# ScalarE issues half of the transfers behind its own results in the first and the last chunk

## The reference

```
x  = _ln(_layernorm(x)); xn = _ln(x); dx = _shift(xn) - xn      # time mixing
r, k, v, decay, a, g from xn + dx * x_q by small matrices
step:  sa    = einsum(state, a_t)                               # 512 steps, one after the other
       state = state * d_t + sa * b_t + v_t * k_t
       o_t   = einsum(state, r_t)
o = _gn_heads(o) + bonus;  x = x + o * g @ W_o
x = x + square(relu(kf @ W_ffn1)) @ W_ffn2                      # first feed-forward
h = _layernorm(x); expert = argmax(h @ W_router)                # second: one of four experts
x = x + _layer_norm(gelu(h @ W1[expert] + b1) @ Wo + bo + h)
```

## Time and profile before

| what | us |
|---|---|
| median of 3 runs | 1193.74 |
| lowest, highest | 1191.18, 1196.12 |
| the profiled execution, its own time | 1195.53 |
| its span, first to last instruction | 1193.7 |
| TensorE busy | 1054.8 (88%) |
| VectorE busy | 940.2 (79%) |
| GpSimd busy | 650.4 (54%) |
| ScalarE busy | 605.3 (51%) |

### The profile page before, as it was taken

One profiled execution on the slowest core, in us unless ns is written; L12 is line 12 of the kernel. 1 busy time (PEld: TensorE's weight loads), 2 busy tenths in 40 slices (PEclk: granted clock), 3 DMA queues, 4 the chain that ended last, 5 costly groups with the idle time before them and its releaser, 6 DMA issues.

```text
span 1193.7 us, 19599 instructions
## 1 busy us (share of the span) xinstructions
PE 1054.8 (88%) x6099; PEld 713.3 (60%) x6099; DVE 940.2 (79%) x2283; ACT 605.3 (51%) x965; POOL 650.4 (54%) x885
## 2 busy tenths in 40 slices
PE   4676689999998999999998989999999999988976
PEld 2243356666565757666665757566666656666755
DVE  4468778898989888898988888898889888876320
ACT  2424364736465574637464564647364654733341
POOL 0246665665656656566656666665556566555200
PEclk9769899999999999999999999999999999999989
DMA  3324123342424233432424232333425233221110
GB/s 126 67 40 75 33 45 71 63 89 42 100 47 86 56 61 69 78 72 52 94 42 96 56 74 56 67 71 62 90 41 102 45 84 57 52 58 36 37 27 18
DMA packets 136496, 75.58 MB, mean 63 GB/s; under 512 B 15292, under 2 KB 129980, under 8 KB 136264
## 3 DMA queue, kind: packets, MB, share of 16 engines
q1 hardware_dynamic: 136392, 74.33, 31.0%
HBM read 11.35 MB, written 4.19 MB: 13 GB/s over the span
## 4 chain that ended last, share of the span: by engine, by line
PE 36%; DVE 20%; SPq 19%; issue 10%; ACT 8%; DMA 6%; POOL 0%; DVEq 0%; ACTq 0%; POOLq 0%
SPq L314 10%; SPq L301 6%; PE fin_b L564 6%; PE fin_a L564 5%; DMA val_rep<-val_c 5%; PE sa_ps L405 5%; DVE state L898 4%; PE mid_ps L356 4%; PE pre_a L356 3%; DVE upd L894 3%; PE var_ps L586 3%; ACT L600 3%; SPq L298 3%; DVE kv L871 2%; DVE s_a L884 1%
## 5 line engine op out<-in xcount | busy, mean ns | idle before, releaser
L1071 POOL TENSOR_TENSOR plus_kv<-state,kv 128x128 f32<-128x128 f32 x512 | 283.3, 553 | 406.1 <-DVE state L898 383.1
L405 PE MATMUL sa_ps<-s_a,con 128*128 128x128 f32 x1024 | 226.0, 303 | 55.8 <-DVE s_a L884 53.2
L405 PEld LDWEIGHTS sa_ps<-s_a,con 128*128 128x128 f32 x1024 | 172.3, 193 | 168.7 <-DVE s_a L884 137.7
L1063 POOL TENSOR_TENSOR s_r<-state,r_t 128x256 f32<-128x256 f32 x256 | 244.7, 956 | 3.3 <-DVE state L898 3.3
L894 DVE TENSOR_TENSOR upd<-sa_ps,b_t 128x128 f32<-128x128 f32 x512 | 146.2, 286 | 84.6 <-PE sa_ps L405 80.7
L898 DVE TENSOR_TENSOR state<-upd,plus_kv 128x128 f32<-128x128 f32 x512 | 191.8, 375 | 17.6
L884 DVE TENSOR_TENSOR s_a<-state,a_t 128x128 f32<-128x128 f32 x512 | 149.4, 292 | 18.5
L564 PE MATMUL fin_b<-h_e,mat 128*128 128x256 f32 x512 | 136.9, 394 | 4.0 <-ACT pick L770 4.0
L871 DVE TENSOR_TENSOR kv<-val_rep,k_t 128x512 f32<-128x512 f32 x128 | 117.8, 921 | 23.9 <-DMA val_rep<-val_c 23.3
L600 ACT ACT_TABLE_LOAD x101 | 129.6, 1283 | 1.8
L564 PE MATMUL fin_a<-h_e,mat 128*128 128x256 f32 x512 | 127.9, 379 | 0.0
(11 more groups left out here) (198 smaller groups left out, 1725.9 us busy)
## 6 DMA issues: line engine op xcount, KB each, us to landing
val_rep<-val_c SPq DMA_DIRECT2D x512, 64.0 KB, 2.4
rs_p<-row_rs SPq DMA_DIRECT2D x128, 64.0 KB, 2.1
x_in<-xT SPq DMA_DIRECT2D x16, 256.0 KB, 3.0
rs_p<-row_rk SPq DMA_DIRECT2D x64, 64.0 KB, 2.4
x_res<-xT SPq DMA_DIRECT2D x16, 256.0 KB, 3.0
rs_m<-row_frs SPq DMA_DIRECT2D x64, 64.0 KB, 2.1
rs_f<-row_ers SPq DMA_DIRECT2D x64, 64.0 KB, 2.1
rs_f<-row_lrs SPq DMA_DIRECT2D x64, 64.0 KB, 2.1
```

The source lines that it names most:

```text
L405: mm(sa_ps[:, 0:STATE], k("sum8"), s_a[:], start=True, stop=True).then_inc(s["sa"], 1)
L1063: tt(part, states, r.unsqueeze(2).broadcast_to([128, 2, N, B]), ALU.mult).then_inc(s["s_r"], 1)
L1071: tt(plus_kv[:, (t % 2) * STATE:(t % 2 + 1) * STATE], st(t), kv[:, at:at + STATE], ALU.add).then_inc(s["plus_kv"], 1)
```

## The change

Every chunk gets a set `by_act`. In chunk 0 it holds rs0, rs1 and rep, in the last chunk ers and lrs, in all others nothing. For a name in the set, SyncE issues only the first half of the DMAs: quarters 0 and 1 of a row of scales, and the first four of the eight of quarter 0 of the values. The second half is issued by ScalarE, from its own queue, right behind the instruction that wrote the row, or val_c. ScalarE waits first for its own result's semaphore and, for the scales, for the last reader of the buffer that is to be overwritten. The number of transfers, their sizes, and the semaphores that their readers wait for stay as they are.

```diff
+        self.by_act = {"rs0", "rs1", "rep"} if off == 0 else {"ers", "lrs"} if off == CHUNKS - 1 else set()
...
                 sp.wait_ge(s["row_" + name], now)
-                for g in range(4):
+                for g in range(2 if name in c.by_act else 4):
...
                 sp.wait_ge(s["val_c"], now)
-                for i in range(N):
+                for i in range(N // 2 if q == 0 and "rep" in c.by_act else N):
...
                 f(row[name][:], row[name][:], ACT.Exp, scale=-0.5).then_inc(s["row_" + name], 1)
+                if name in c.by_act:
+                    to, read, back = {"rs0": (rs_p, "kk", 1), "rs1": (rs_p, "xh0", 0),
+                                      "ers": (rs_f, "lxh", 1), "lrs": (rs_f, "h", 0)}[name]
+                    if c.has(back):
+                        act.wait_ge(s[read], (c + -back).count())
+                    act.wait_ge(s["row_" + name], c.count())
+                    for g in (2, 3):
+                        rows = row[name][32 * g:32 * g + 32, :].unsqueeze(1).broadcast_to([32, 4, QCOLS])
+                        nc.scalar.dma_start(to[:, g * QCOLS:(g + 1) * QCOLS], rows).then_inc(s[name], 16)
...
                     f(val_c[:], pre_a[:], ACT.Identity).then_inc(s["val_c"], 1)
+                    if "rep" in c.by_act:
+                        act.wait_ge(s["val_c"], c.count())
+                        for i in range(N // 2, N):
+                            heads = val_c[i * H:(i + 1) * H, 0:QCOLS].unsqueeze(1).broadcast_to([H, N, QCOLS])
+                            nc.scalar.dma_start(val_rep[0][:, i * QCOLS:(i + 1) * QCOLS], heads).then_inc(s["val_rep0"], 16)
```

## The result

| | median, us | lowest to highest | runs |
|---|---|---|---|
| before | 1196.60 | 1191.18 to 1200.14 | 20 |
| after | 1189.85 | 1186.86 to 1194.27 | 20 |

The ratio of after to before is 0.9948, with a 95% interval of 0.9937 to 0.9959. Of 1196 us that is 6.2 us less, 4.9 to 7.5. The two medians lie 6.75 apart, which is inside this interval. The forecast, 1187.5 against a median of 1193.74, was a ratio of 0.9948 and 6.2 us. The median of before has moved up by 2.9 us with more runs; the ratio is what compares.

What follows compares the result with a forecast made beforehand. Bound taken as the chain of waits, its largest item SyncE issuing DMAs, in the first and last chunks. Gains 0.84 + 1.15 + 1.9 + 2.3 = 6.2 us take the median 1193.74 to 1187.5, range 1184.2 to 1194.6.

Steps and rivals of the forecast that it cites:

- rs1: Second row of scales in chunk 0: nothing else is late, so the whole saving of 1.15 us counts.
- quarter 0, load of x: Values and x load in chunk 0: pre_a<-x_in starts at 54.75 instead of 56.66, gain 1.9 us, low end 1.1.
- ers: Row of scales in the last chunk: half issued by ScalarE, holding it costs nothing, gain 1.15 us.
- lrs: Other row of scales in the last chunk: same pattern, gain 1.15 us, 2.3 together with ers.
- Pitch and side by side: ScalarE issues every 0.64 us beside SyncE; shared engines cost 0 to 0.27, taken as 0.13, leaving 1.15 a row.
- rs0 held by the keep matmuls: Chunk 0: TensorE's keep matmuls run until 16.43, so pre_a starts there, not at 16.12; gain 0.84 us.
- k_t ends at 47.4: VectorE in chunk 0: k_t is only 0.45 us late, so kv starts at 47.6 instead of 50.19.
- They are the new bound: TensorE's keep matmuls end at 52.65, later than s_a at 51.9, so scan step 0 starts at 52.65 instead of 53.73.
- The middle passes the shift through: From 60 to 1148 us no instruction changes and everything hangs on semaphores, so the early gain carries to the end.
- Rival A: Both queues share what sets the pitch, so rows gain nothing; price 0 to 0.7 us, 1193.7 to 1194.4; chance 0.27.
- Rival B: Shorter wait behind ers may leave TensorE's clock up; 2.6 us more gained, 1184.9; chance 0.15.
- Rival C: An issue costs ScalarE much more, 1.81 us; rows and val_c lose 6.9 us together, 1200.6; chance 0.08.

Runs made afterwards that it cites:

- all_again: The whole changed kernel run once more with nothing altered, beside its parts; 1190.14 us, ratio 0.9949 to before.
- scales0: Changed kernel cut to rs0 and rs1 of chunk 0, quarter 0 and the last chunk as before; 1192.72 us, ratio 0.9974 to before.
- tail_only: Changed kernel cut to ers and lrs of the last chunk issued half by ScalarE; 1193.28 us, ratio 0.9976 to before.
- act_alone: Against the changed kernel, ScalarE issues all four transfers of rs0, rs1, ers and lrs, values stay with SyncE; 1195.86 us, ratio 0.9994 to before.
- rep_only: Changed kernel cut to quarter 0 of the values in chunk 0 issued half by ScalarE; 1194.26 us, ratio 0.9983 to before.
- rep_every: Changed kernel plus quarter 0 of the values issued half by ScalarE in every chunk; 1249.74 us, ratio 1.0448 to before.
- rep_two: Changed kernel, but ScalarE issues two of the eight transfers of quarter 0 in chunk 0, not four; 1188.87 us, ratio 0.9943 to before.
- rs1_every: Changed kernel plus rs1 issued half by ScalarE in every chunk; 1184.81 us, ratio 0.9899 to before.

## Why the prediction was right, point by point

**The sum** was 6.2 us, with ends of 4.9 and 7.7. Measured are 6.2, between 4.9 and 7.5. The upper end takes rs0 at 1.28, though by the forecast itself the keep matmuls stop it at 0.84. Its terms, from the distances in the traces:

| term | forecast | measured |
|---|---|---|
| rs0 | 0.84 | 1.0 |
| rs1 | 1.15 | 1.05 |
| quarter 0, load of x | 1.9 | 0.9 to 1.2; 0.4 in after |
| ers | 1.15 | 0.84 to 0.9 |
| lrs | 1.15 | 1.2 to 1.3 |
| sum | 6.2 | 5.0 to 5.45 |

The sum leaves out the 0.4 of after. The terms sum to 0.75 to 1.2 less than the ratio says, so that the forecast meets it to the tenth is in part luck; the interval takes in both.

**Pitch and side by side: right.** ScalarE's issues have SyncE's pitch of 0.64, and the two overlap. The last of rs0 landed 3.12 us after its row, where the forecast looked for 2.9. The cost of sharing was put at 0.13, with 0.27 as the end. It measured 0.27 to 0.4, so a row of scales gains around 1.0, not 1.15. For rk and the values the forecast had two transfers take 0.80 us of the engines' time every 0.64 us, more than there is; measured, the engines were 0.81 busy from 38.4 to 42.3 us in all_again.

**rs0 held by the keep matmuls: right, and worth little.** In scales0, TensorE's timeline:

```profile
14.15 2.05 PE L588 MATMUL var_ps<-con 128*128 128x256 f32 x4
16.20 2.07 PE L358 MATMUL pre_a<-x,con 128*128 128x512 f32 x2
```

pre_a starts when the keep matmuls end. The row-to-pre_a distance fell from 5.81 to 4.79, by 1.02; the room was a little wider than the forecast's 0.84.

**Quarter 0 and the load of x: the term was mis-sized, 1.9 for 0.9 to 1.2, and a step in it failed.** Positions are taken from val_c's start: 40.26 in before, 38.17 in scales0, 36.73 in all_again. val started 0.48 later in all_again, as forecast (0.45). Step 0 was to move from 13.47 to 12.39, held by the keep matmuls. It moved to 13.30 in all_again, held by VectorE, and to 14.22 in after, held by the keep matmuls. What failed is the step "k_t ends at 47.4", which let k_t start only 0.45 late, and the two operations behind it at 0.7 each: the backlog of the DMA engines was put at 0.6 and none of it was charged to rk, whose transfers land at the same time. mix_v came 1.02 to 1.07 later, and this put k_t and kv beside GpSimd, at 1.75 and 1.64. "They are the new bound", of the keep matmuls, failed with it wherever TensorE's clock was up in that stretch; in after, where it was not, they were the bound, but of a step 0 that came later than in before and not earlier. As forecast, the load of x no longer made TensorE wait, and pre_a<-x_in follows step 1: 51.94 - 36.73 = 15.21, against 16.40 in before and 14.49 in the forecast. Against before this is 1.2, of which step 0 gave 0.17 and the load the rest. The other kernels that leave quarter 0 whole (scales0, tail_only, act_alone) have 16.12 to 16.16, against which it is 0.9; in after it is 16.03, a gain of 0.4 against before. The forecast's own low end for this term, 1.1, was the better value.

**The middle passes the shift through: right in sum, not in every profile.** SyncE's loads and stores at the same places of the two profiles lie 6.6 us apart at 106 us, 4.3 at 240, 4.1 at 912, 1.9 at 1108, 3.2 at 1150 and 4.0 at the end. The first number is too large for the change. In all_again, the same kernel, the same places lie 5.4, 6.9, 6.3, 5.9, 7.2 and 8.2 us ahead of before. In after the early matmuls ran at the full clock (below), which took VectorE's weight work out of the way, and the second xh_p came 3.86 us earlier than before instead of 2. This was given back later, where TensorE's mean granted clock was lower than in before: 0.92 against 0.94 from 100 to 240 us, 0.97 against 1.00 from 1040 to 1106. In all_again it was 0.95 and 1.00, and its profile ended at 1185.5, 4.2 below that of after. One pair of profiles can't size a change of 6 us; the runs and the local distances do.

**Rival A, one generator for both queues: refuted.** While both issued, ScalarE's issues took 0.60 to 0.62, SyncE's 2.63 for four. By A an issue would have taken 1.2 on each queue. The Trainium skill's "Perfetto Trace Analysis", section "DMA Instruction — HWDGE (DVE, Sync)", has the block that makes descriptors shared and locked for one DMA at a time. If that lock held between these two queues, act_alone and the split rows would take the same time; they differ by about 1 us a row. "DMA: Bandwidth & Descriptors", section "Issuing engines are not separate DMA queues", says that several issuers save the sequencer's time and interleave on the same 16 engines. The trace agrees with this one: the pitch was saved, and the last landing came at 2.40 to 2.54 instead of 2.13.

**Rival B, the clock stays up behind ers: refuted.** Stretches of 2 us of after, to be held against the earlier trace rows; PEclk stands third from the end:

```profile
1152.00:1154.00 2.00, 1.13 (x8) 1.04 (x8) 0.68 (x5) 0.00 (x0) 0.00 (x0) 0.73 0.00 0
1154.00:1156.00 2.00, 1.51 (x15) 1.52 (x16) 0.83 (x5) 0.00 (x0) 0.00 (x0) 0.50 0.00 0
```

The clock still fell to half (1.2 GHz) behind the wait, though that was 0.84 us shorter. The first sixteen matmuls of the experts took 6.09 in after, 5.23 in all_again, 6.45 in tail_only, against 5.46 in before and 5.73 and 6.73 in scales0 and rep_only, which don't touch ers. This varies by over 1.2 us from one execution to the next, on either side.

**Rival C, ScalarE issues at a much higher price: refuted** by 0.58 to 0.67 for each issue and by act_alone, which lost nothing. Where ScalarE's results are waited for, though, the ordinary price is enough for a loss: 2.93 us of issues a chunk cost rep_every 4.5%.

## What to carry to other kernels

A spread of n DMAs that a chain waits for ends earlier by the issues that a second queue takes over at the same time, here 0.64 us each, less the 0.3 to 0.4 by which the last transfer then lands later; moving all of them to the other queue gains nothing. Before an engine is made to issue, look at what stands behind the issue in its queue and who waits for that: two issues a chunk in front of a table load gained 1.0% in all, four in front of the scan's feeders cost 4.5%. And of an added burst, ask what other transfer is on its way at that moment, and what the reader of that one will run beside.

## What the runs showed of the hardware

**Matmuls at half clock under a PEclk of 1.00.** From 16 to 18 us the stretches show PEclk 1.00, in after and in all_again:

```profile
16.00:18.00 2.00, 2.00 (x11) 1.21 (x10) 1.90 (x6) 0.79 (x3) 0.00 (x0) 1.00 0.00 0
```

```profile
16.00:18.00 2.00, 2.00 (x3) 0.84 (x3) 1.90 (x6) 0.14 (x1) 0.00 (x0) 1.00 0.00 0
```

The same pre_a of two matmuls took 1.09 in after and 2.02 in all_again, 2.07 in before. By their lengths, the second ran at half the clock. So early in the span the matmul's duration says what the clock was, and the printed figure doesn't. Which of the two an execution gets was not steered by any of the edits: only the profile of after had it from 16 us on; in the others this pre_a took 1.80 to 2.08.

**VectorE beside GpSimd.** The same TENSOR_TENSOR of 128x512 in f32 took 0.68 alone and 1.63 to 1.75 with GpSimd's TENSOR_TENSOR beside it, and GpSimd's mix_k 1.71 where it took 1.26 in before. In these rows k_t goes by which of the two starts first: in before k_t started 0.30 us ahead of GpSimd's r_t, and in rep_two 0.10 ahead, and took 0.68 though the two overlap; in rep_only it started 0.25 behind and took 1.75.

**Open.** The local gains sum to 5.0 to 5.45, the ratio says 6.2; the difference is within the interval and wasn't pursued. How the gain of rs1_every divides between VectorE's shorter wait for the values (9.7 us less) and the earlier second normalization (ScalarE's xn waited 32.9 us instead of 48.3) wasn't taken apart.
